# Macaron block (mixture of experts, attention, mixture of experts) on one core: another order of the opening

## The chip, the cores and the metric

The kernel runs on one NeuronCore of a Trainium2 chip. It is one launch; the time is the device time in microseconds of that core, and lower is better. The core has five engines that run side by side, each with its own instruction stream: TensorE (PE) multiplies matrices, VectorE (DVE) and ScalarE (ACT) work element by element and can read the PSUM banks into which TensorE writes, GpSimd (POOL) works element by element on SBUF, and SyncE (SP) issues data transfers (DMAs). An engine takes its instructions in the written order, and waits on semaphores for the others.

## The reference, cut to what matters

`x` has 8 sequences of 1024 tokens with 128 features, in float32. The output is made in three steps.

```
x = x + 0.5 * ffn(layernorm(x))
x = x + attention(layernorm(x))        # causal, one head, d = 128
x = x + 0.5 * ffn(layernorm(x))        # the same weights as in the first

def ffn(f):                            # f: 8192 tokens x 128
    scores = sigmoid(f @ Wg.T)         # 16 experts, in 4 groups of 4
    topk_idx, topk_w = route(scores, bias_corr)   # 2 best groups, in them the 4 best experts,
                                       # weights divided by their sum, times 2.5
    cw = zeros(T, 16).at[..., topk_idx].add(topk_w)
    hid = relu(einsum('th,eih->eti', f, W1)) ** 2     # 64 hidden units per expert
    out = einsum('eth,te->th', einsum('eti,ehi->eth', hid, W2), cw)
    return out + relu(f @ Ws1.T) ** 2 @ Ws2.T         # plus a shared expert of 128 units
```

## The kernel before, in words

All tokens stay in SBUF (`x_sb`: 64 tiles of 128 tokens). An expert phase goes through 16 groups of 4 tiles (512 tokens). The hidden units are cut into 9 chunks of 128: chunks 0 to 7 hold two experts each, chunk 8 is the shared expert. Chunk m counts on over the groups, so that group 2 begins with chunk 18. For each chunk:

- `up` (L1268): TensorE multiplies the chunk of W1 with the group's normalised, transposed tokens. Float32 precision comes from three products of rounded values (`split3`, L1205): high by high, high by low, low by high. There are three PSUM banks for it (HB = 3), so up m waits for gate m - 3.
- `gate` (L950): VectorE takes the positive part and multiplies it with `wb`, the square root of the routing weight of each token, spread over the partitions (L958); for the shared expert there is no weight (L960). Gates of chunks 0 and 4 of a group wait for the two halves of the load of `wb`.
- `square` (L516): ScalarE squares into a rounded high half (L521) and a full one (L522).
- `lo_part` (L380): POOL subtracts the two (L385). Chunk 5 of a group has no such part and is multiplied in full precision (L1280).
- `down` (L1275): TensorE multiplies with the chunk of W2 and adds up in PSUM.

TensorE runs `up` four chunks ahead of `down` (AHEAD = 4). Between them stand the preparing steps of later groups: statistics (L766, L773, L777), a power of -1/2 on POOL for the standard deviation (L368, `inv`) and for the routing sum (L378, `norm_root`), `norm_shift` (L797), `normalise` (L466 on ScalarE, L812 on VectorE), transposes (L1238), a copy to `x_f`, a rounded copy `x_hi` (L452 in both cases: the line of the helper `copy`), `x_lo` on POOL (L391), logits, and the routing in ten parts (L817 to L947; the last writes `scw`, L946). Its result is transposed (L1266), copied to `wT` on ScalarE, stored to memory by SP (L310), and loaded back in a spread form into `wb` (L323): four transfers of 512 KB a group, 2 MB. SP waits for the store to land before it issues the loads, and waits for `wT` of the next group. All of SP's transfers go through one queue.

The opening (on TensorE `opening` at L1295, on ScalarE at L528, on VectorE at L977, on POOL in `start` at L406) prepares groups 0 to 3 and the weights, and starts chunks 0 to 3. SP's queue holds first the tokens of groups 0 and 1, the first weights, groups 2 and 3, then all other tokens in one transfer of 3 MB (L298), then Qw, Kw and Vw; ScalarE's queue holds W2 and Ws2 (L454). TensorE transposes the weights in five sets of four squares (`weights_transpose`, L1211): sets 0 and 1 are W1, 2 and 3 are W2, set 4 is the shared expert and Qw, Kw. ScalarE copies each set from PSUM to a rounded high half (`weights_hi`, L697), and VectorE makes the low half by subtracting that from PSUM (`weights_lo`, L745). Each of groups 1 to 3 has its first two tiles normalised by ScalarE (`first_half`) and the other two by VectorE (`second_half`). The shift of a group can only be written when the tiles of the group before are normalised (L795, and L395 on POOL for the power).

## Time and profile before

| | |
|---|---|
| Time, median of 3 runs | 699.76 us (699.64 to 699.94) |
| The profiled execution's own time | 699.16 us |
| Its span in the profile | 697.4 us |
| TensorE busy | 668.6 us, 96% |
| VectorE busy | 562.0 us, 81% |
| ScalarE busy | 536.0 us, 77% |
| POOL busy | 438.3 us, 63% |
| Moved by DMA | 78.37 MB, 112 GB/s over the span |

Times in the rows are microseconds from the start of the span. A bracket at the end of a row tells for how long the engine did nothing ahead of the instruction, and the arrow which instruction or transfer ended that. SPq and ACTq are the issuing of transfers; a transfer lands later. The first expert phase lasts until about 245 us, attention until about 488 us, the second expert phase until the end.

### The profile page before, as it was taken

To read this page: it belongs to the slowest core of one execution; us is meant where nothing else is said; L and a number is where in the kernel's file an instruction comes from. 1 tells how busy PE (TensorE), PEld (TensorE's weight loads), DVE (VectorE), ACT (ScalarE), POOL (GpSimd) and SP (SyncE) were. 2 spreads that over 40 slices of the span, in tenths; PEclk is the share of its full clock that TensorE was granted. 3 is DMA by queue.
4 is the path that set the end of the run, shared out by engine and by line. 5 is a ranking of instruction groups with operands and counts; after the bars stand their busy time and mean duration, and the time that the engine had idled before them with its cause. 6 is when DMAs were issued, how large, how long until landed. Compare 5 with 4: busy or idle time off the path is not lost.

```text
span 697.4 us, 15216 instructions
## 1 busy us (share of the span) xinstructions
PE 668.6 (96%) x3395; PEld 507.7 (73%) x3395; DVE 562.0 (81%) x2586; ACT 536.0 (77%) x1122; POOL 438.3 (63%) x347
## 2 busy tenths in 40 slices
PE   4789999999999997999999999999999999999997
PEld 3567777777777775787778777767777777777775
DVE  5898988889888885666656678898888899888863
ACT  3479889888898866675566477669898888988975
POOL 3379888989899972000000021148889988999975
PEclk9999999999999999999999999999999999999999
DMA  9867777667775740000000000264887787867783
GB/s 245 195 128 149 151 160 154 126 141 154 162 151 124 157 86 1 1 1 1 0 1 0 0 1 0 57 135 101 167 172 157 166 176 173 166 143 176 162 175 81
DMA packets 53525, 78.37 MB, mean 112 GB/s; under 512 B 5216, under 2 KB 19184, under 8 KB 53488
## 3 DMA queue, kind: packets, MB, share of 16 engines
q1 hardware_dynamic: 51280, 77.36, 51.7%
q10 hardware_dynamic: 2208, 0.59, 0.4%
q8 instruction: 14, 0.23, 0.1%
q14 instruction: 23, 0.19, 0.1%
HBM read 72.70 MB, written 5.24 MB: 112 GB/s over the span
## 4 chain that ended last, share of the span: by engine, by line
PE 76%; DVE 13%; ACT 5%; issue 4%; POOL 1%; DMA 1%; DVEq 0%; POOLq 0%; ACTq 0%
PE psum L1207 19%; PE psum L1208 18%; PE psum L1209 18%; PE psum L1430 6%; PE psum L1280 4%; DVE nmax L1087 3%; PE psum L1238 2%; PE psum L1419 2%; PE psum L1292 2%; ACT shared L630 2%; PE psum L1443 2%; DVE zn L1101 2%; PE psum L1254 1%; DVE s_sb L958 1%; ACT wb L452 1%
## 5 line engine op out<-in xcount | busy, mean ns | idle before, releaser
L385 POOL TENSOR_TENSOR shared_r<-shared,shared_r 128x512 fp32r<-128x512 f32 x256 | 326.7, 1299 | 54.3 <-ACT shared L522 51.7
L958 DVE SCALAR_TENSOR_TENSOR s_sb<-psum,wb 128x512 f32<-128x512 f32 x256 | 175.7, 688 | 46.3 <-DMA wb<-scratch 22.0
L521 ACT ACTIVATE shared_r<-s_sb 128x512 fp32r<-128x512 f32 x256 | 160.2, 626 | 44.1 <-DVE s_sb L958 43.0
L522 ACT ACTIVATE shared<-s_sb 128x512 f32<-128x512 f32 x288 | 178.0, 620 | 18.5 <-DVE s_sb L958 18.5
L1207 PE MATMUL psum<-x_hi,w_hi 128*128 128x512 f32 x288 | 127.6, 443 | 0.9 <-DVE x_sb L1113 0.5
L1207 PE MATMUL psum<-shared_r,w_hi 128*128 128x512 f32 x256 | 114.2, 446 | 0.8 <-POOL shared_r L385 0.7
L1208 PE MATMUL psum<-x_lo,w_hi 128*128 128x512 f32 x288 | 114.7, 398 | 0.0
L1209 PE MATMUL psum<-x_hi,w_lo 128*128 128x512 f32 x288 | 114.3, 397 | 0.0
L1208 PE MATMUL psum<-shared_r,w_hi 128*128 128x512 f32 x256 | 101.0, 395 | 0.0
L1209 PE MATMUL psum<-shared_r,w_lo 128*128 128x512 f32 x256 | 100.9, 394 | 0.0
L368 POOL TENSOR_TENSOR a_rstd<-a_mv,neg_half 128x8 f32<-128x8 f32 x8 | 13.1, 1638 | 116.5 <-DVE a_mv L777 116.5
L1207 PEld LDWEIGHTS psum<-x_hi,w_hi 128*128 128x128 f32 x288 | 54.7, 190 | 20.7 <-issue 7.2
L1208 PEld LDWEIGHTS psum<-x_lo,w_hi 128*128 128x128 f32 x288 | 54.7, 190 | 18.2 <-issue 7.2
L630 ACT ACTIVATE shared<-psum,nmax 128x128 f32<-128x128 f32 (+3 forms) x64 | 47.5, 742 | 23.6 <-DVE nmax L1087 22.3
L1209 PEld LDWEIGHTS psum<-x_hi,w_lo 128*128 128x128 f32 x288 | 54.6, 189 | 13.1
L1087 DVE TENSOR_REDUCE nmax<-psum 128x1 f32<-128x128 f32 (+3 forms) x64 | 47.5, 752 | 19.8 <-PE psum L1410 19.7
L1207 PEld LDWEIGHTS psum<-shared_r,w_hi 128*128 128x128 f32 x256 | 48.2, 188 | 18.7 <-issue 5.5
L466 ACT ACTIVATE xn<-x_sb,shift,roots 128x128 f32 (+1 forms) x128 | 55.6, 482 | 2.8 <-DVE shift L797 2.7
L1209 PEld LDWEIGHTS psum<-shared_r,w_lo 128*128 128x128 f32 x256 | 48.1, 188 | 10.9
L1208 PEld LDWEIGHTS psum<-shared_r,w_hi 128*128 128x128 f32 x256 | 48.6, 190 | 5.0 <-issue 0.2
L404 POOL TENSOR_TENSOR roots<-powers,neg_half 128x8 f32<-128x8 f32 x28 | 45.9, 1638 | 6.4 <-DVE powers L938 5.3
L1430 PE MATMUL psum<-wb,zn 128*128 128x512 f32 (+3 forms) x128 | 47.2, 513 | 0.0
(173 smaller groups left out, 1276.4 us busy)
## 6 DMA issues: line engine op xcount, KB each, us to landing
wb<-scratch SPq DMA_DIRECT2D x128, 512.0 KB, 8.3
out<-x_sb SPq DMA_DIRECT2D x16, 256.0 KB, 9.9
x_sb<-in_L_attn_x SPq DMA_DIRECT2D x4, 256.0 KB, 6.2
scratch<-wT SPq DMA_DIRECT2D x32, 32.0 KB, 1.9
w_raw<-in_L_ffn_W ACTq DMA_DIRECT2D x1, 512.0 KB, 6.0
w_raw<-in_L_ffn_W SPq DMA_DIRECT2D x1, 512.0 KB, 6.7
w_raw<-in_L_ffn_Ws ACTq DMA_DIRECT2D x1, 64.0 KB, 8.7
w_raw<-in_L_ffn_Ws SPq DMA_DIRECT2D x1, 64.0 KB, 7.3
```

Source lines behind the costliest of these rows:

```text
L385: nc.gpsimd.tensor_tensor(g_lo[:, j % RING, :], g_f[:, j % RING, :], g_hi[:, j % RING, :].bitcast(F32), ALU.subtract).then_inc(F.glo_done, 1)
L404: nc.gpsimd.tensor_tensor(roots[:], powers[:], neg_half[:, 0:2 * TG], ALU.pow).then_inc(F.rstd_done, 1)
L466: ins = nc.scalar.activation(xn[:, t, :], x_sb[:, bass.ds(g * TG + t, 1), :].rearrange("p t d -> p (t d)"), ACT.Identity, bias=shift[:, t: ...
L521: nc.scalar.activation(g_hi[:, j % RING, :], s_sb[:, j % RING, :], ACT.Square)
L522: nc.scalar.activation(g_f[:, j % RING, :], s_sb[:, j % RING, :], ACT.Square).then_inc(F.sq_done, 1)
L630: nc.scalar.activation(prob[:, t % PR, 0:w], sc_ps[t % 2][:, 0:w], ACT.Exp, bias=nmax[:, u, t:t + 1], accum_out=rsum[:, u, t:t + 1]).then_ ...
L958: ins = nc.vector.scalar_tensor_tensor(s_, h_, 0.0, wb[:, u, c, :], ALU.max, ALU.mult)
L1087: nc.vector.tensor_reduce(nmax[:, u, t:t + 1], sc_ps[t % 2][:, 0:(t + 1) * P], AX.X, ALU.max, negate=True).then_inc(A.max_done, 1)
L1207: mm(out_, l_hi, r_hi, start=start, stop=False)
L1208: mm(out_, l_hi, r_lo, start=False, stop=False)
L1209: return mm(out_, l_lo, r_hi, start=False, stop=stop)
L1430: ins = mm(u_ps[:, q0:], zn[:, u, k, :], pT[half][:, k, q0:], start=(k == 0), stop=(k == last - 1))
```

## The change

- SP's first transfer (tiles 0 to 3) becomes two of two tiles; the second is issued by ScalarE. W2 and Ws2 move from ScalarE's queue to SP's, behind the tokens of group 3.
- The 3 MB of other tokens become three transfers: group 4 behind Vw; groups 5 and 6 behind the `wb` load of group 0; groups 7 to 15 behind the `wb` load of group 1. VectorE waits for the second before the body of groups 0 and 1 and for the third before the loop that follows.
- `weights_lo` moves from VectorE to POOL. POOL doesn't read PSUM, so ScalarE copies each set once more, unrounded, to SBUF (`wt_f`, in the space of `zn` and `oT`).
- Groups 1 to 3 are normalised by ScalarE alone (`whole_group`).
- TensorE transposes set 4 and the first routing weights earlier, and makes up 0 and 1 ahead of the transposes of group 2, and up 2 ahead of those of group 3. The first down waits for all low halves.
- VectorE, ScalarE and POOL get a new order in the opening.

```diff
@@ -224,6 +224,8 @@
         pT = [w_raw[:, 0:HQ * HQ * P].rearrange("p (k q) -> p k q", k=HQ),
...
         uT = s_sb[:, AHEAD:AHEAD + 2, :]
+        zn_flat = zn[:].rearrange("p u t d -> p (u t d)")
+        wt_f = [zn_flat[:, 512 * w:512 * (w + 1)] for w in range(4)] + [oT[:]]
...
         up_ps = [psum[:, b, :] for b in range(HB)]
@@ -261,8 +263,9 @@
         N_SETS = len(wt_ps)
-        x_in = [sem(f"x_in{g}") for g in range(4)]
-        x_rest = sem("x_rest")
+        x_in = [sem(f"x_in{g}") for g in range(5)]
+        x_rest = [sem(f"x_rest{n}") for n in range(2)]
+        XR = (5, 7, NG)
         wg_in, bias_in, w1_in, w2_in, small_in = sem("wg_in"), sem("bias_in"), sem("w1_in"), sem("w2_in"), sem("small_in")
...
         wgT_done, wgT_copied = sem("wgT_done"), sem("wgT_copied")
@@ -286,7 +289,7 @@
         def _(sp):
-            sp.dma_start(x_sb[:, 0:TG, :], x_v[:, 0:TG, :]).then_inc(x_in[0], 16)
+            sp.dma_start(x_sb[:, 0:TG // 2, :], x_v[:, 0:TG // 2, :]).then_inc(x_in[0], 16)
             sp.dma_start(wg_raw[:], Wg).then_inc(wg_in, 16)
...
             w1_rows = W1.rearrange("e i h -> (e i) h").rearrange("(c p) h -> p c h", p=P)
@@ -295,10 +298,13 @@
             sp.dma_start(bias_bc[:], bias_corr.rearrange("(a e) -> a e", a=1).broadcast_to([P, E])).then_inc(bias_in, 16)
...
                 sp.dma_start(x_sb[:, TG * g:TG * (g + 1), :], x_v[:, TG * g:TG * (g + 1), :]).then_inc(x_in[g], 16)
-            sp.dma_start(x_sb[:, 4 * TG:NT, :], x_v[:, 4 * TG:NT, :]).then_inc(x_rest, 16)
+            sp.dma_start(w2_raw[:, NC, :], Ws2).then_inc(w2_in, 16)
+            sp.dma_start(w2_raw[:, 0:NC, :].rearrange("h c (j i) -> h (c j) i", i=I),
+                         W2.rearrange("e h i -> h e i")).then_inc(w2_in, 16)
             sp.dma_start(qk_raw[:, 0, :], Qw).then_inc(small_in, 16)
...
             sp.dma_start(vw[:], Vw).then_inc(small_in, 16)
+            sp.dma_start(x_sb[:, 4 * TG:5 * TG, :], x_v[:, 4 * TG:5 * TG, :]).then_inc(x_in[4], 16)
...
                 F = FF[phase]
@@ -329,6 +335,9 @@
                     spread(n, n % UN)
+                    if phase == 0 and n < 2:
+                        cs = slice(TG * XR[n], TG * XR[n + 1])
+                        sp.dma_start(x_sb[:, cs, :], x_v[:, cs, :]).then_inc(x_rest[n], 16)
                     if phase == 1 and n == 2 * UN - 1:
...
                 with sp.Fori(2, NG // UN) as i:
@@ -370,6 +379,19 @@
             def attention_inv(b):
...
+            def weights_lo(w):
+                pool.wait_ge(wt_hi, w + 1)
+                flat = lambda a, k: a[:, 4 * k:4 * k + 4, :].rearrange("p c n -> p (c n)")
+                lo_of = lambda lo, hi, f: nc.gpsimd.tensor_tensor(lo, f, hi.bitcast(F32), ALU.subtract)
+                if w < 2:
+                    lo_of(flat(w1_lo, w), flat(w1_hi, w), wt_f[w]).then_inc(wt_lo, 1)
+                elif w < 4:
+                    lo_of(flat(w2_lo, w - 2), flat(w2_hi, w - 2), wt_f[w]).then_inc(wt_lo, 1)
+                else:
+                    lo_of(w1_lo[:, NC, :], w1_hi[:, NC, :], wt_f[w][:, 0:P])
+                    lo_of(w2_lo[:, NC, :], w2_hi[:, NC, :], wt_f[w][:, P:2 * P]).then_inc(wt_lo, 1)
             def ffn(F):
...
@@ -408,15 +430,22 @@
                     inv(1)
...
                         x_lo_part(0, 0)
+                        weights_lo(0)
                         norm_root(0)
                         inv(2)
+                        weights_lo(1)
                     else:
...
                         norm_root(0)
+                    if F is FF[0]:
+                        weights_lo(2)
+                    inv(3)
+                    if F is FF[0]:
+                        weights_lo(3)
+                        weights_lo(4)
                     x_lo_part(1, 1)
-                    inv(3)
                     norm_root(1)
...
                         lo_part(m, m)
@@ -451,9 +480,7 @@
         def _(sc):
...
-            sc.dma_start(w2_raw[:, 0:NC, :].rearrange("h c (j i) -> h (c j) i", i=I),
-                         W2.rearrange("e h i -> h e i")).then_inc(w2_in, 16)
-            sc.dma_start(w2_raw[:, NC, :], Ws2).then_inc(w2_in, 16)
+            sc.dma_start(x_sb[:, TG // 2:TG, :], x_v[:, TG // 2:TG, :]).then_inc(x_in[0], 16)
...
             nc.scalar.activation(warm[:], neg_half[:], ACT.Sigmoid)
@@ -525,6 +552,10 @@
                     for t in range(TG // 2):
...
+                def whole_group(n):
+                    for t in range(TG):
+                        normalise(F, n, t)
                 def opening():
                     first_half(0)
@@ -532,24 +563,24 @@
                     copy(wgT[:, 0:E], lg_ps[:, 0:E]).then_inc(wgT_copied, 1)
...
                     sigmoid(0, 0, lg_ps)
-                    first_half(1)
+                    whole_group(1)
                     x_hi_copy(0, 0)
...
                     weights_hi(2)
+                    wT_copy(0, wT_ps)
                     weights_hi(3)
+                    weights_hi(4)
                     x_hi_copy(1, 1)
-                    wT_copy(0, wT_ps)
-                    first_half(2)
+                    whole_group(2)
                     x_copy(2, 0, tr_ps)
                     sigmoid(2, 0, lg_ps)
-                    weights_hi(4)
-                    first_half(3)
-                    x_copy(3, 1, tr_ps)
+                    whole_group(3)
                     attention_matrix()
                     lead(0)
+                    x_copy(3, 1, tr_ps)
                     wT_copy(1, wT_ps)
...
                         lead(c)
@@ -700,15 +731,18 @@
                 src = wt_ps[w]
...
                 if w < 2:
-                    copy(flat(w1_hi, w), src).then_inc(wt_hi, 1)
+                    copy(flat(w1_hi, w), src)
+                    copy(wt_f[w], src).then_inc(wt_hi, 1)
                 elif w < 4:
...
                             copy(w2_f[:, n, :], src[:, (c % 4) * P:(c % 4 + 1) * P])
-                    copy(flat(w2_hi, w - 2), src).then_inc(wt_hi, 1)
+                    copy(flat(w2_hi, w - 2), src)
+                    copy(wt_f[w], src).then_inc(wt_hi, 1)
                 else:
...
                     copy(w2_hi[:, NC, :], src[:, P:2 * P])
+                    copy(wt_f[w][:, 0:2 * P], src[:, 0:2 * P])
                     copy(qkT[:].rearrange("p c n -> p (c n)"), src[:, 2 * P:4 * P]).then_inc(wt_hi, 1)
             def attention_matrix():
@@ -741,19 +775,6 @@
             nc.vector.memset(scw[:, E:, :], 0.0).then_inc(FF[0].stat, 1)
...
             v.wait_ge(FF[0].stat, n_const)
-            def weights_lo(w):
-                v.wait_ge(wt_hi, w + 1)
-                src = wt_ps[w]
-                flat = lambda a, k: a[:, 4 * k:4 * k + 4, :].rearrange("p c n -> p (c n)")
-                if w < 2:
-                    tt(flat(w1_lo, w), src, f32(flat(w1_hi, w)), ALU.subtract).then_inc(wt_lo, 1)
-                elif w < 4:
-                    tt(flat(w2_lo, w - 2), src, f32(flat(w2_hi, w - 2)), ALU.subtract).then_inc(wt_lo, 1)
-                else:
-                    tt(w1_lo[:, NC, :], src[:, 0:P], f32(w1_hi[:, NC, :]), ALU.subtract)
-                    tt(w2_lo[:, NC, :], src[:, P:2 * P], f32(w2_hi[:, NC, :]), ALU.subtract).then_inc(wt_lo, 1)
...
@@ -977,30 +998,25 @@
                 def opening():
                     def statistics(n):
-                        v.wait_ge(x_in[n], 16)
+                        v.wait_ge(x_in[n], 32 if n == 0 else 16)
                         stats(n, range(TG))
...
                     statistics(1)
-                    second_half(1)
+                    norm_shift(1)
                     v.wait_ge(bias_in, 16)
...
                     route_parts(0, 9)
-                    weights_lo(0)
-                    weights_lo(1)
-                    second_half(2)
+                    route_parts(1, 0, 1)
+                    norm_shift(2)
                     statistics(3)
-                    route_parts(1, 0, 1)
-                    weights_lo(2)
-                    weights_lo(3)
-                    second_half(3)
-                    route_parts(1, 2)
-                    weights_lo(4)
-                    route_parts(1, 3, 4, 5, 6, 7, 8)
-                    v.wait_ge(x_rest, 16)
+                    route_parts(1, 2, 3, 4)
+                    norm_shift(3)
+                    route_parts(1, 5, 6, 7, 8)
+                    v.wait_ge(x_in[4], 16)
                     for c in range(AHEAD):
...
@@ -1057,7 +1073,11 @@
                             extra(j)
                 def run(first_extra, last_extra):
+                    if phase == 0:
+                        v.wait_ge(x_rest[0], 16)
                     body(0, True, False, first_extra)
+                    if phase == 0:
+                        v.wait_ge(x_rest[1], 16)
                     if phase == 1:
...
                     with v.Fori(1, NG // UN - 1) as i:
@@ -1275,6 +1295,8 @@
                 def down(g, c, m, j, u):
...
                         wait(pe, F.oT_copied, g - 1)
+                        if phase == 0 and isinstance(g, int) and g == 0:
+                            pe.wait_ge(wt_lo, N_SETS)
                     if c in WHOLE:
...
                         mm(o_ps[u], w2_f[:, WHOLE.index(c), :], g_f[:, j % RING, :], start=(c == 0),
@@ -1306,20 +1328,23 @@
                     xn_transpose(1, tr_ps)
...
                     weights_transpose(2)
+                    w_transpose(0, wT_ps, sigmoids=2)
                     weights_transpose(3)
-                    w_transpose(0, wT_ps, sigmoids=2)
+                    weights_transpose(4)
+                    pe.wait_ge(wt_lo, 1)
+                    pe.wait_ge(wt_hi, 2)
+                    lead(0)
+                    lead(1)
                     pe.wait_ge(F.xf_done, 2)
...
                     logits(2, 0, lg_ps, wT_copied=1)
-                    weights_transpose(4)
+                    pe.wait_ge(wt_hi, N_SETS)
+                    lead(2)
+                    attention_matrix()
                     pe.wait_ge(F.xf_done, 3)
                     xn_transpose(3, tr_ps)
-                    pe.wait_ge(wt_hi, N_SETS)
-                    pe.wait_ge(wt_lo, N_SETS)
-                    attention_matrix()
-                    for c in range(AHEAD - 1):
-                        lead(c)
                     w_transpose(1, wT_ps, sigmoids=3)
+                    pe.wait_ge(wt_lo, 2)
                     pe.wait_ge(m_copied, 2)
...
```

## Rows read from the trace of the kernel before

**Rows 1.** Busy time by stages: us, then per engine busy (instructions), PEclk, DMA share, GB/s

```profile
34.80:43.00 8.20, 6.16 (x33) 3.96 (x31) 7.95 (x54) 5.05 (x10) 5.41 (x6) 1.00 0.66 143
43.00:245.00 202.00, 201.75 (x991) 154.04 (x992) 180.33 (x900) 179.54 (x380) 182.72 (x141) 1.00 0.70 147
```

**Rows 2.** Waits of TensorE, 43 to 245 us, and its timeline where that begins

```profile
PE psum L1259 <- ACT lgT L452: 1.9, 2, 1.7
...
42.89 0.33 PE L1259 MATMUL psum<-ident,lgT 128*128 128x128 f32 x1 [1.66 <-ACT lgT L452]
```

**Rows 3.** Timeline of the opening: start, duration, engine, line, instruction, count

```profile
4.74 0.87 DVE L766 BATCH_NORM_STATS2 bn<-x_sb 128x6 f32<-128x128 f32 x4 [1.31 <-DMA x_sb<-in_L_attn_x]
...
19.32 0.26 DVE L946 SCALAR_TENSOR_TENSOR scw<-psum,roots 128x64 f32<-128x64 f32 x1
...
19.64 0.48 PE L1266 MATMUL psum<-ident,scw 128*128 128x128 f32 x1 [0.32 <-DVE scw L946]
...
20.53 0.26 ACT L452 ACTIVATE wT<-psum 64x128 f32<-64x128 f32 x1
...
20.82 0.55 SPq L310 DMA_DIRECT2D scratch<-wT  x1
...
23.96 2.64 SPq L323 DMA_DIRECT2D wb<-scratch  x4
```

**Rows 4.** Timeline and lines: what moves between engines, and where gate 1 stands

```profile
13.77 0.58 ACT L452 ACTIVATE w_hi<-psum 128x512 fp32r<-128x512 f32 x1
...
20.72 1.26 POOL L391 TENSOR_TENSOR x_lo<-x_f,x_hi 128x512 fp32r<-128x512 f32 x1 [0.22 <-ACT x_hi L452]
...
20.84 0.88 ACT L466 ACTIVATE xn<-x_sb,shift,roots 128x128 f32<-128x128 f32 x2
20.84 1.48 DVE L812 TENSOR_SCALAR xn<-x_sb,roots,shift 128x128 f32<-128x128 f32 x2
...
24.71 1.28 DVE L753 TENSOR_TENSOR w_lo<-psum,w_hi 128x512 fp32r<-128x512 f32 x2
...
33.19 0.68 DVE L958 SCALAR_TENSOR_TENSOR s_sb<-psum,wb 128x512 f32<-128x512 f32 x1
...
L812 DVE TENSOR_SCALAR xn<-x_sb,roots,shift x16: 334/344/1223, 7.6 to 452.8; 128x128 f32<-128x128 f32 x16
...
L933 DVE SCALAR_TENSOR_TENSOR chosen<-marked,scores x32: 217/419/1241, 17.2 to 656.7; 128x64 f32<-128x64 f32 x32
```

**Rows 5.** Busy time by short stretches, for the DMA columns at the end

```profile
10.00:20.00 10.00, 8.53 (x37) 7.58 (x37) 7.63 (x58) 4.86 (x12) 3.56 (x4) 1.00 1.07 292
35.00:36.00 1.00, 1.00 (x6) 0.82 (x5) 1.00 (x7) 0.59 (x2) 0.33 (x1) 1.00 0.37 71
47.00:48.00 1.00, 1.00 (x7) 0.76 (x6) 0.99 (x7) 1.00 (x3) 0.57 (x2) 1.00 0.88 162
```

**Rows 6.** Timeline: stores and loads of groups 1 and 2, gate 18, down 19

```profile
34.58 0.52 SPq L310 DMA_DIRECT2D scratch<-wT  x1
36.88 3.09 SPq L323 DMA_DIRECT2D wb<-scratch  x4
51.05 0.52 SPq L310 DMA_DIRECT2D scratch<-wT  x1
52.92 2.57 SPq L323 DMA_DIRECT2D wb<-scratch  x4
...
60.70 0.69 DVE L958 SCALAR_TENSOR_TENSOR s_sb<-psum,wb 128x512 f32<-128x512 f32 x1
...
68.34 0.50 PE L1207 MATMUL psum<-shared_r,w_hi 128*128 128x512 f32 x1
```

**Rows 7.** Timeline: a first gate of a group that is late

```profile
148.38 0.69 DVE L958 SCALAR_TENSOR_TENSOR s_sb<-psum,wb 128x512 f32<-128x512 f32 x1 [1.70 <-DMA wb<-scratch]
...
150.34 1.30 POOL L385 TENSOR_TENSOR shared_r<-shared,shared_r 128x512 fp32r<-128x512 f32 x1 [1.62 <-ACT shared L522]
...
152.85 5.07 POOL L385 TENSOR_TENSOR shared_r<-shared,shared_r 128x512 fp32r<-128x512 f32 x4
```

## What the change does to the time: the prediction

> **What bounds the kernel now.** I read the busy time by stages first. From 43 us to the end of the first expert phase TensorE is busy for 201.75 of 202.00 us [rows 1], and all that it waits for there is 1.9 us behind one copy of ScalarE, nearly all of it once, ahead of 42.89 us [rows 2]. So from about 43 us on the kernel is a fixed amount of TensorE work, and the end moves by as much as TensorE is earlier or later at any place after that. Before it, in 34.8 to 43 us, VectorE is busy for 7.95 of 8.20 us and TensorE for 6.16 [rows 1]: the opening is paced by VectorE. The diff touches the opening and the loads. An opening that is x us shorter is worth x us, if nothing behind it is late. I therefore read next what must be on time behind it: the broadcast loads of the routing weights (wb, 2 MB a group), one after another in SP's queue. Their times were 23.96, 36.88 and 52.92 us [rows 3, 6].
>
> I call gate m the VectorE instruction that makes the gated activation of chunk m (9 chunks a group), up m the product that it reads and down m the product that needs it. Gate 18 is the first of group 2.
>
> **The change part by part.**
>
> *First tokens in two halves, W2 away from ScalarE's queue.* VectorE could start at 3.4 us, and starts at 4.74 because it waited 1.31 us for 256 KB that shared the engines with 512 KB of W2 [rows 3]. Alone, this data should land earlier. Bounds: 0 and 1.3 us; I take 0.9, since transfers run at up to 292 GB/s [rows 5], so that removing some 250 KB of interleaved data is worth 0.9.
>
> *The chain to the first wb load.* VectorE's part (statistics, routing of group 0, `scw` at 19.32) keeps its order. The copy of wT stood behind x_hi_copy(1) and ran at 20.53, though the transpose of `scw` was done at 20.12 [rows 3]. Now it stands behind weights_hi(2), which by the copy's 0.58 us [rows 4] ends about when the transpose does: 0.3 us gained. The store then goes out at 20.82 - 0.9 - 0.3 = 19.6. In the trace it took until 23.96 because 3 MB of tokens were ahead of it in the queue; with an empty queue it takes 51.05 to 52.92, 1.9 us [rows 3, 6]. So the first wb load is issued at **21.5** in place of 23.96.
>
> *Low halves of the weights on POOL.* Off VectorE go four subtractions of 0.64 us (1.28 for two) and two small ones, some 3.1 us; with them six normalise instructions [rows 4]. ScalarE gets the six (0.44 us each, 0.88 for two) and five copies more of 0.58 or less, some 5.2 us. POOL gets five instructions of up to 1.3 us, a time that its subtraction shows at that size [rows 4], some 5.9 us, and norm_root(1) and inv(3) now stand behind them. Both lists fit in the opening, with the order below. down of chunk 0 waits for all of them, over 5 us after they are done by this count.
>
> *Where this puts gate 1.* ScalarE after wT_copy(0) at 19.5: 0.7 wait, weights_hi(3) and (4) 2.5, x_hi 0.6, four normalises 1.6: 24.9. Then transposes of group 2, copy, logits, sigmoid 3.9: 28.8; four normalises and the copies of the attention matrix 2.5: 31.3; VectorE's m_lo 0.3. Gate 1 is at 31.6 in place of 33.19 [rows 4]. On POOL inv(3) starts at 24.9, then three subtractions and norm_root(1) end at 30.2, so it is no later. From gate 1 on VectorE's list is the old one, so the whole of TensorE's stream would be **1.6 us earlier**. Bounds: nothing (POOL and ScalarE just late enough) and 3 us (all of VectorE's relief).
>
> *Up products ahead of two groups' transposes.* TensorE is not the limit there, so placing up 0 to 2 early gives nothing by itself and costs nothing: they fill its waits.
>
> *A port rule.* Beside a POOL subtraction some VectorE instructions stretch: two normalises took 1.48 us against 0.60, one of them up to 1223 ns against a median of 344, and L933, which reads two SBUF tiles, has 217 to 1241 ns [rows 4]. The Trainium skill, "SBUF — State Buffer", section "SBUF: two separate sides", says why: VectorE's two-port modes, or its instructions with two SBUF inputs, and a GpSimd instruction hold a shared pair of ports exclusively, each for a whole instruction. The trace agrees. It speaks against the change, because weights_lo(0) (about 15.0 to 16.3) ends just where L933 of group 0 falls (16.3), on the chain to the first wb load; by that rule it could lose up to 1.3 us. In the sum I count none and put 1.3 into the upper bound; the normalises that lost 1.1 us are now ScalarE's.
>
> *The tokens behind the wb loads.* Here the cost is. Groups 7 to 15, 36 tiles or 2.36 MB, are issued straight behind the load of group 1, and the store and load of group 2 stand behind them in the same queue. The queue works in order: the store at 34.58 was not in before 36.88, 1.5 us after the last bytes of group 0's load (flow tails off at 35.4) [rows 5, 6]. The count:
> - group 0's load flows until 11.4 us after its issue (23.96 to 35.4) [rows 3, 5]: 32.9. Half a megabyte of tokens behind it at 292 GB/s: 34.7. The store of group 1, issued by 33.5, lands 1.5 later: 36.2 (36.88 before).
> - group 1's load flows until 11.0 after its issue (36.88 to 47.9) [rows 5, 6]: 47.2. Then 2.36 MB at 288 GB/s: 8.2 us, 55.4. Before, the engines were idle here until 52.9. The store of group 2, issued since 49.5, lands at 56.9.
> - gate 18 can run 7.8 us after the issue (52.92 to 60.70) [rows 6]: **64.7**. Before: 60.70, with the load just in. So it is 4.0 us later than before.
>
> *What that costs.* The trace has a late gate of this kind: 148.38, waiting on the load. POOL's low half followed at 150.34, after it the x_lo of the next group and the low half of chunk 19, whose successor starts at 152.85 + 1.25 [rows 7]. So down 19 can't start before gate 18 + 5.9 (with 0.15 for the signal). In group 2 it starts at 68.34 [rows 6], 7.6 after its gate: 1.7 us of slack beyond the 5.9. New start: 64.7 + 5.9 = 70.6, **2.3 us later than before**. This is not added to the 1.6: TensorE comes to this place 1.6 us early, waits 3.9, and leaves 2.3 late. The load of group 3 follows its own store about 10 us after it, moves along with the engines and adds nothing.
>
> **Sum.** The profiled execution took 699.16 us for a span of 697.4; with +2.3 it is 701.4. The median of the runs, 699.76, is 0.6 above the profile: 702.0. Taking the bounds together (the first load 0.4 earlier to 2.2 later, transfers 0.5 us either way, the slack 0.5 either way) the likeliest case alone is 700.8 to 704.6.
>
> **Rivals.**
> 1. *The loads are in time* and only the opening counts: 1.6 us, 698.2 (with its bounds 696.8 to 699.8). For it: the count needs seven legs in a row, and gate 18 may slip 1.7 us free. If the legs come out 4 us shorter (packets of the two transfers overlapping, tokens quicker at 2.36 MB), TensorE never waits. Against: engines are already at a share of 1.07 while moving tokens [rows 5], so nothing overlaps for free.
> 2. *Both nearly cancel:* the late load costs back about the gain, which it does if the first wb load is issued near 19.5 or if the store of group 2 is issued ahead of part of the tokens. End within 1.4 us of before: 699.8.
> 3. *POOL makes the opening longer* (the other side even with loads in time): ports held on VectorE at each of the five subtractions, and norm_root(1) behind x_lo(1). It decides when norm_root(1) ends after 31.8 (its old start) plus 1; five holds of up to 1.2 us would push gate 1 to 34.5 and, through the store of group 1, everything in the count by 2 us more: 704.
> 4. *The change doesn't do what it says:* the first tokens land no sooner, since the delay is latency and not bandwidth. Then all of it is 0.9 later: 702.9, inside the range.
>
> **Chances.** Likeliest case with rival 4: 0.50. Rival 1: 0.22. Rival 2: 0.20. Rival 3: 0.08. A measurement of this kernel tells 0.2% (1.4 us) from no change. Slower by more: most of the first and the third, 0.52; within: 0.26; faster by more: 0.22. Predicted 701.9 us, with the range 697.8 to 704.6.
>
> **What would show it.** Right: first statistics near 3.8 us; store of group 0 near 19.6, its load issued near 21.5; gate 1 near 31.6; x_sb's last transfer landing at 55 or later and SP's load of group 2 issued near 57; a wait of VectorE on wb of 3 us or more ahead of gate 18 near 64.7, and a wait of TensorE of 3 to 4 us near 65 to 70. Wrong: the load of group 2 issued before 55, no wait of TensorE behind 43 us, or gate 1 later than 33.

## The result, and the profile after

The changed kernel takes 703.83 us (median of 8 runs, 701.78 to 705.05), the kernel before beside it 699.82 us (8 runs, 698.47 to 700.71): a ratio of 1.005 with a 95% interval of 1.0033 to 1.0067, so 2.3 to 4.7 us slower; the two medians are 4.0 us apart. It was run once more later, against more runs of before: 1.0045 (1.003 to 1.006). The profiled execution took 705.05 us for a span of 703.2 us; it is the slowest of the eight. The prediction said 701.9, in 697.8 to 704.6.

Lines have moved by some twenty: the gate is L979, the three `up` products L1227 to L1229, the pair that begins `down` of chunk 5 L1302, the store L316, the `wb` load L329.

First the opening, which answers to [rows 3, 4]. This is the timeline of the kernel after (start, duration, engine, line, instruction, count, and in brackets the idle time before it and what ended it):

```profile
3.71 0.87 DVE L787 BATCH_NORM_STATS2 bn<-x_sb 128x6 f32<-128x128 f32 x4 [0.29 <-DMA x_sb<-in_L_attn_x]
...
19.12 0.27 ACT L481 ACTIVATE wT<-psum 64x128 f32<-64x128 f32 x1
...
19.42 0.59 SPq L316 DMA_DIRECT2D scratch<-wT  x1
21.32 2.68 SPq L329 DMA_DIRECT2D wb<-scratch  x4
24.05 0.84 SPq L340 DMA_DIRECT2D x_sb<-in_L_attn_x  x1
...
29.14 0.69 DVE L979 SCALAR_TENSOR_TENSOR s_sb<-psum,wb 128x512 f32<-128x512 f32 x1 [1.22 <-DMA wb<-scratch]
30.08 0.69 DVE L979 SCALAR_TENSOR_TENSOR s_sb<-psum,wb 128x512 f32<-128x512 f32 x1
...
39.78 0.33 PE L1279 MATMUL psum<-ident,lgT 128*128 128x128 f32 x1 [1.51 <-ACT lgT L481]
```

The first four rows are as predicted (3.8, then 19.6 for the store and 21.5 for the load). Gate 1 is at 30.08 and not 31.6, and TensorE's wait for `lgT`, the last of the opening, ends at 39.78 where it ended at 42.89 [rows 2]: the opening is 3.1 us shorter, not 1.6.

Then the loads behind it, answering to [rows 6], and the busy time by stretches (per engine busy time and instructions in the order TensorE, its weight loads, VectorE, ScalarE, POOL; then TensorE's granted clock, DMA share, GB/s), answering to [rows 1]:

```profile
36.71 2.59 SPq L329 DMA_DIRECT2D wb<-scratch  x4
39.76 0.78 SPq L340 DMA_DIRECT2D x_sb<-in_L_attn_x  x1
47.93 5.43 SPq L316 DMA_DIRECT2D scratch<-wT  x1
57.18 2.60 SPq L329 DMA_DIRECT2D wb<-scratch  x4
...
64.76 0.69 DVE L979 SCALAR_TENSOR_TENSOR s_sb<-psum,wb 128x512 f32<-128x512 f32 x1 [7.31 <-DMA wb<-scratch]
```

```profile
34.80:43.00 8.20, 6.69 (x35) 4.96 (x35) 7.75 (x48) 5.85 (x13) 6.57 (x6) 1.00 0.63 141
43.00:245.00 202.00, 197.53 (x958) 150.22 (x957) 172.83 (x869) 173.73 (x369) 176.15 (x136) 0.98 0.73 154
49.00:56.00 7.00, 7.00 (x40) 5.28 (x39) 6.26 (x33) 6.07 (x13) 7.00 (x6) 1.00 1.06 289
60.00:65.00 5.00, 1.46 (x9) 0.89 (x7) 0.24 (x1) 0.00 (x0) 0.00 (x0) 0.96 1.05 214
65.00:71.00 6.00, 5.49 (x13) 4.33 (x14) 5.83 (x37) 5.51 (x12) 4.29 (x4) 0.50 0.62 120
```

TensorE lost 4.5 us in a phase where it had lost 0.25. From 49 to 56 us the engines move tokens at 289 GB/s, and the store of group 2, issued at 47.93, is behind them (its issuing alone takes 5.43 us, 0.52 in before [rows 6]): its load goes out at 57.18 (predicted 56.9), and gate 18 runs at 64.76 (predicted 64.7). The last row holds what was not predicted: from 65 to 71 us the granted clock is 0.50, the lower of its two levels (1.2 of 2.4 GHz). TensorE's timeline shows what that is in matmuls:

```profile
61.06 0.40 PE L1229 MATMUL psum<-shared_r,w_lo 128*128 128x512 f32 x1
65.51 0.79 PE L1227 MATMUL psum<-x_hi,w_hi 128*128 128x512 f32 x1 [4.05 <-DVE s_sb L979]
66.10 0.63 PE L1228 MATMUL psum<-x_lo,w_hi 128*128 128x512 f32 x1
66.53 0.63 PE L1229 MATMUL psum<-x_hi,w_lo 128*128 128x512 f32 x1
...
70.79 0.63 PE L1227 MATMUL psum<-x_hi,w_hi 128*128 128x512 f32 x1
71.22 0.52 PE L1228 MATMUL psum<-x_lo,w_hi 128*128 128x512 f32 x1
71.58 0.39 PE L1229 MATMUL psum<-x_hi,w_lo 128*128 128x512 f32 x1
71.89 0.43 PE L1274 MATMUL psum<-x_f,wgT 128*32 128x128 f32 x8
72.25 0.50 PE L1227 MATMUL psum<-shared_r,w_hi 128*128 128x512 f32 x1
```

Behind the wait of 4.05 us the matmuls start 0.43 us apart, until 71.2; then 0.23 again. The last row is down 19, at 72.25: 3.9 us later than before [rows 6], where 2.3 was predicted.

One place serves as a marker in every run below: the start of `down` of chunk 5, the only matmul in two products. In TensorE's timeline it starts for groups 0, 1 and 2 at 45.85, 60.22, 74.58 before, and at 42.73, 57.11, 78.48 after: 3.1 early, 3.1 early, 3.9 late. For the last group it is 688.77 and 694.69, 5.9 late. A group takes 14.35 us, and nine of the thirteen profiles, that of before too, have single groups that take 0.5 to 1.2 more, at other places in each (before, group 8 starts 14.85 after group 7). The 3.9 grow by 2.0 to the 5.9. Two such groups in the kernel after and one in before make 0.7 of that, 0.6 come between 237 and 494 us, 0.5 in the last groups. In the second profile of the changed kernel (below) it is 3.8 at the end.

What makes a group slow can be read from the timeline, here that of before between the markers of groups 7 and 8:

```profile
155.66 1.07 DVE L933 SCALAR_TENSOR_TENSOR chosen<-marked,scores 128x64 f32<-128x64 f32 x1
156.66 0.68 DVE L958 SCALAR_TENSOR_TENSOR s_sb<-psum,wb 128x512 f32<-128x512 f32 x1
157.37 0.63 ACT L522 ACTIVATE shared<-s_sb 128x512 f32<-128x512 f32 x1 [1.23 <-DVE s_sb L958]
157.91 0.26 ACT L452 ACTIVATE lgT<-psum 128x128 f32<-128x128 f32 x1
158.22 0.33 PE L1259 MATMUL psum<-ident,lgT 128*128 128x128 f32 x1 [0.25 <-ACT lgT L452]
```

L933, a step of the routing that reads two SBUF tiles, starts inside the third of four POOL subtractions in a row [rows 7] and takes 1.07 us where it can take 0.22. The gate behind it is late, ScalarE waits 1.23 us for the gate, its copy `lgT` is late, and TensorE waits. Of the groups that have a routing, 16 in all profiles together take 14.8 us or more without a late load; each of these has this instruction at 0.66 to 1.26 us and a wait of TensorE for `lgT` of 0.20 to 0.54. The reverse doesn't hold: the instruction also takes up to 1.40 us in groups of 14.35.

### The profile page after: what moved, and what is told of

It reads as the page before. It is cut to its first block, busy times and chain, and to the rows that moved or that the text cites. A ratio compares the mean times of both kernels' runs of the same rounds, so it can differ in the third digit from the quotient of the medians.

```text
span 703.2 us, 15219 instructions
## 1 busy us (share of the span) xinstructions
PE 672.4 (96%) x3395; PEld 509.4 (72%) x3395; DVE 558.4 (79%) x2574; ACT 539.6 (77%) x1133; POOL 443.4 (63%) x353
## 4 chain that ended last, share of the span: by engine, by line
PE 64%; DVE 13%; DMA 8%; ACT 6%; issue 5%; POOL 2%; SPq 0%; DVEq 0%; POOLq 0%; ACTq 0%
PE psum L1227 16%; PE psum L1228 15%; PE psum L1229 15%; PE psum L1455 6%; DMA wb<-scratch 5%; PE psum L1302 3%; DVE nmax L1107 2%; DVE s_sb L979 2%; DMA scratch<-wT 2%; PE psum L1444 2%; ACT shared L661 2%; PE psum L1468 2%; PE psum L1258 2%; PE psum L1314 2%; DVE zn L1121 1%
## 5 line engine op out<-in xcount | busy, mean ns | idle before, releaser
L979 DVE SCALAR_TENSOR_TENSOR s_sb<-psum,wb 128x512 f32<-128x512 f32 x256 | 175.2, 687 | 53.9 <-DMA wb<-scratch 32.7
L1227 PE MATMUL psum<-x_hi,w_hi 128*128 128x512 f32 x288 | 128.6, 446 | 4.4 <-DVE s_sb L979 4.0
L1227 PE MATMUL psum<-shared_r,w_hi 128*128 128x512 f32 x256 | 115.1, 450 | 1.2 <-POOL shared_r L407 1.2
L1229 PE MATMUL psum<-x_hi,w_lo 128*128 128x512 f32 x288 | 115.3, 400 | 0.0
L1229 PE MATMUL psum<-shared_r,w_lo 128*128 128x512 f32 x256 | 101.6, 397 | 0.0
L1227 PEld LDWEIGHTS psum<-x_hi,w_hi 128*128 128x128 f32 x288 | 55.2, 192 | 23.9 <-issue 6.7
L661 ACT ACTIVATE shared<-psum,nmax 128x128 f32<-128x128 f32 (+3 forms) x64 | 47.4, 741 | 23.1 <-DVE nmax L1107 21.9
L1229 PEld LDWEIGHTS psum<-x_hi,w_lo 128*128 128x128 f32 x288 | 55.1, 191 | 13.2
L1227 PEld LDWEIGHTS psum<-shared_r,w_hi 128*128 128x128 f32 x256 | 48.7, 190 | 19.0 <-issue 5.0
L493 ACT ACTIVATE xn<-x_sb,shift,roots 128x128 f32 (+1 forms) x134 | 57.8, 483 | 4.1 <-DVE shift L818 4.1
L1229 PEld LDWEIGHTS psum<-shared_r,w_lo 128*128 128x128 f32 x256 | 48.6, 190 | 11.1
```

The costliest lines, as they stand in the source:

```text
L493: ins = nc.scalar.activation(xn[:, t, :], x_sb[:, bass.ds(g * TG + t, 1), :].rearrange("p t d -> p (t d)"), ACT.Identity, bias=shift[:, t: ...
L661: nc.scalar.activation(prob[:, t % PR, 0:w], sc_ps[t % 2][:, 0:w], ACT.Exp, bias=nmax[:, u, t:t + 1], accum_out=rsum[:, u, t:t + 1]).then_ ...
L979: ins = nc.vector.scalar_tensor_tensor(s_, h_, 0.0, wb[:, u, c, :], ALU.max, ALU.mult)
L1227: mm(out_, l_hi, r_hi, start=start, stop=False)
L1229: return mm(out_, l_lo, r_hi, start=False, stop=stop)
```

## The experiments

The theory after the result: *the late load of group 2 makes the kernel slower, and hides an opening that is 3.1 us shorter*. The rival: *something else of the change costs it*, VectorE's or POOL's new lists, or the clock. All times are given beside before on the same chip. The first four ran beside 27 runs of before with a median of 701.9 us, 5 to 8 beside 29 with 700.69, 9 to 11 beside 22 with 700.23; so ratios are compared, and the markers.

**1. Tokens in the gaps.** The change, with groups 5 to 11 moved into the idle queue of the opening, group 12 behind load 0 and only 13 to 15 behind load 1.

```diff
-        XR = (5, 7, NG)
+        XR = (5, 12, 13, NG)
...
             sp.dma_start(x_sb[:, 4 * TG:5 * TG, :], x_v[:, 4 * TG:5 * TG, :]).then_inc(x_in[4], 16)
+            sp.dma_start(x_sb[:, TG * XR[0]:TG * XR[1], :], x_v[:, TG * XR[0]:TG * XR[1], :]).then_inc(x_rest[0], 16)
```

> The changed kernel with its tokens placed elsewhere: groups 5 to 11 straight behind group 4, in the stretch from 12.4 to 19.4 us in which its trace moves nothing, group 12 behind the load of group 0, groups 13 to 15 (0.79 MB, 2.7 us) behind the load of group 1. Theory L (the late load of group 2 is the whole loss): the store of group 2 lands about when it did before relative to the engines, gate 18 near 58, no wait of TensorE of over 0.5 us behind 43 us, granted clock 1.00 from 35 us on; the opening's 3.1 us stay: 696.7 us, ratio to before 0.9955. Rival O (POOL and ScalarE, loaded with more, cost later, and the load only covers it): 699 to 703 us.

Measured: 698.99 us, ratio 0.9973 (0.9956 to 0.999), the profiled execution 697.94. The load of group 2 and gate 18 in its timeline:

```profile
50.30 2.58 SPq L330 DMA_DIRECT2D wb<-scratch  x4
...
58.06 0.69 DVE L980 SCALAR_TENSOR_TENSOR s_sb<-psum,wb 128x512 f32<-128x512 f32 x1 [0.50 <-DMA wb<-scratch]
```

Nothing else was changed, and TensorE no longer waits there; the clock is 1.00 from 34 us on. The marker is 3.0 us earlier than before in all of the first groups (42.84, 57.22, 71.57). Of that 1.2 are left at the last group of the profile (687.58 against 688.77), behind groups of 14.92, 15.11 and 14.69 us; the ratio forecast, 0.9955, was not reached. So the kernel that was slower becomes faster, by the place of one transfer alone. That shows the theory's first half.

**2. Before, with the tokens late and nothing else** (group 4 alone in the opening, 5 and 6 behind load 0, 7 to 15 behind load 1, and the waits for them).

```diff
-            sp.dma_start(x_sb[:, 4 * TG:NT, :], x_v[:, 4 * TG:NT, :]).then_inc(x_rest, 16)
+            sp.dma_start(x_sb[:, 4 * TG:5 * TG, :], x_v[:, 4 * TG:5 * TG, :]).then_inc(x_in[4], 16)
...
                     spread(n, n % UN)
+                    if phase == 0 and n < 2:
+                        cs = slice(TG * XR[n], TG * XR[n + 1])
+                        sp.dma_start(x_sb[:, cs, :], x_v[:, cs, :]).then_inc(x_rest[n], 16)
```

> The kernel before with one part of the change alone: group 4 behind group 3, groups 5 and 6 behind the load of group 0, groups 7 to 15 behind the load of group 1. Theory L: store of group 0 lands at 22.7 in place of 23.96, the store of group 2 at about 58, gate 18 near 65.7 against 60.7; TensorE waits some 2 us ahead of up 21. If its clock stays at 1.00 the end is 3.3 us later (703.1), if the wait drops it to 0.5 for as long as in the changed kernel, 4.8 us later (704.6). Rival O: within 1 us of before, since engines have their old lists.

Measured: 705.49 us, ratio 1.0072 (1.0043 to 1.0101); marker 45.65, 60.03, 78.71, the last 4.1 late. The load of group 2 went out at 57.97. The wait by itself is 2.5 us, and here too the clock falls, 1.5 us after TensorE has started again, and stays low until 71.4:

```profile
66.88 0.50 PE L1215 MATMUL psum<-x_hi,w_hi 128*128 128x512 f32 x1 [2.50 <-DVE s_sb L962]
67.22 0.40 PE L1216 MATMUL psum<-x_lo,w_hi 128*128 128x512 f32 x1
...
68.15 0.43 PE L1217 MATMUL psum<-shared_r,w_lo 128*128 128x512 f32 x1
68.38 0.63 PE L1215 MATMUL psum<-x_hi,w_hi 128*128 128x512 f32 x1
```

So the tokens' place costs 4 us by itself. The profiled execution, 702.63 us, is the fastest of the five. As ratios the two expectations are 1.0047 (clock kept) and 1.0068 (clock lost): the second is met, the first isn't excluded.

**3. The wait filled.** The change, with 34 transposes of the identity, written where nothing is read any more, ahead of up 21: TensorE works through its wait. They are extra work, 3.87 us in all.

```diff
+                                if phase == 0 and first and j == UN * NCH - 1:
+                                    for _ in range(34):
+                                        nc.tensor.transpose(o_ps[0][:, 0:P], ident[:], ident[:])
                                 up(g + 1, (c + AHEAD) % NCH, m + AHEAD, (j + AHEAD) % (UN * NCH), 0)
```

> The changed kernel, and in the 4 us wait ahead of up 21 TensorE makes 34 transposes that nobody reads (3.7 us by 0.11 us each), into a bank that is free then. Theory L with the clock: the time of the wait is the load's and stays, but TensorE's granted clock stays at 1.00 in 65 to 71 us, where the changed kernel has 0.50, so down 19 comes 2.7 us sooner: 701.1 us against 703.8. Rival (the 6.7 us from up 21 to down 19 are POOL's chain and not the clock): at least 1.7 us of them stay and the time is 702.8 or more.

Measured: 704.06 us, ratio 1.0054 (1.0033 to 1.0075), the profiled execution 703.68. The same stretch of TensorE:

```profile
61.75 3.87 PE L1381 MATMUL psum<-ident 128*128 128x128 f32 x34
65.38 0.47 PE L1227 MATMUL psum<-x_hi,w_hi 128*128 128x512 f32 x1
65.69 0.40 PE L1228 MATMUL psum<-x_lo,w_hi 128*128 128x512 f32 x1
...
69.85 0.43 PE L1274 MATMUL psum<-x_f,wgT 128*32 128x128 f32 x8 [0.43 <-ACT x_f L481]
70.24 0.50 PE L1227 MATMUL psum<-shared_r,w_hi 128*128 128x512 f32 x1
```

The clock stays at 1.00, and down 19 is at 70.24 behind a gate 18 at 64.43: 5.8 us, the predicted distance of 5.9. In the kernel after it was 7.5. But the marker of group 2 is at 77.24, only 1.2 ahead of the kernel after, and 0.36 of that is a load that went out earlier. From down 19 to the marker it is 6.24 us in before and 6.23 in the kernel after, and 7.00 here, because this group is one of the slow ones: L954 takes 1.05 us at 71.73, and TensorE waits for `lgT`:

```profile
74.27 0.33 PE L1279 MATMUL psum<-ident,lgT 128*128 128x128 f32 x1 [0.53 <-ACT lgT L481]
```

The times don't tell the two apart: the intervals 1.0033 to 1.0075 and 1.0033 to 1.0067 lie on each other. At the marker 0.9 us of the low clock's cost came back. With the usual 6.24 the marker would be at 76.5, so I estimate its cost at 1.6 us; whether the slow group stands there in every execution, one profile doesn't tell. The expected 701.1 was wrong: with the clock back the marker is still 2.7 us later than before (1.9 by that estimate), and a group of 15.47 us comes later.

**4. All tokens ahead of the first store.** The change, with groups 5 to 15 as one transfer in the opening.

```diff
+            sp.dma_start(x_sb[:, 5 * TG:NT, :], x_v[:, 5 * TG:NT, :]).then_inc(x_rest[0], 16)
...
-                    if phase == 0 and n < 2:
-                        cs = slice(TG * XR[n], TG * XR[n + 1])
-                        sp.dma_start(x_sb[:, cs, :], x_v[:, cs, :]).then_inc(x_rest[n], 16)
```

> The changed kernel with all tokens of groups 5 to 15 ahead of the first store, as the kernel before has them. Theory L: the store of group 0, issued at 19.4, lands behind them near 23.9, the first gate is at 31.7 in place of 29.1, later loads are in time, no wait behind 43 us. Of the opening's 3.1 us some 0.5 are left: 699.3 us. Rival O: 702 us or more.

Measured: 703.87 us, ratio 1.003 (1.0007 to 1.0052); a miss. Store and load of group 0, the gate behind them, and two stretches of five:

```profile
19.30 3.00 SPq L317 DMA_DIRECT2D scratch<-wT  x1
26.00 2.65 SPq L330 DMA_DIRECT2D wb<-scratch  x4
...
33.99 0.69 DVE L977 SCALAR_TENSOR_TENSOR s_sb<-psum,wb 128x512 f32<-128x512 f32 x1 [6.17 <-DMA wb<-scratch]
```

```profile
10.00:15.00 5.00, 4.06 (x19) 3.29 (x18) 3.40 (x29) 3.80 (x10) 1.44 (x2) 1.00 0.66 166
28.00:34.00 6.00, 1.08 (x4) 0.71 (x4) 0.01 (x1) 1.02 (x4) 1.48 (x2) 0.50 1.05 223
```

Before, the engines moved 292 GB/s from 10 to 20 us [rows 5]; here it is 166 from 10 to 15, while SP's queue is at W2, whose transfer now stands in it. The expectation took over the 23.9 of before; the tokens end later, the store is behind them, and the load goes out at 26.00, 4.7 after the kernel after. TensorE waits 5.3 us for `scw` and works at the lower clock until about 41 us. The marker of group 2 (76.31) is 1.7 late. It is a second case of the same fault, at another group.

**5 to 8. One part of experiment 1 taken back in each**, to find what the 3.0 us come from.

*5: the first tokens whole on SP again, W2 and Ws2 on ScalarE's queue.*

```diff
-            sp.dma_start(x_sb[:, 0:TG // 2, :], x_v[:, 0:TG // 2, :]).then_inc(x_in[0], 16)
+            sp.dma_start(x_sb[:, 0:TG, :], x_v[:, 0:TG, :]).then_inc(x_in[0], 16)
...
-            sc.dma_start(x_sb[:, TG // 2:TG, :], x_v[:, TG // 2:TG, :]).then_inc(x_in[0], 16)
+            sc.dma_start(w2_raw[:, 0:NC, :].rearrange("h c (j i) -> h (c j) i", i=I),
+                         W2.rearrange("e h i -> h e i")).then_inc(w2_in, 16)
```

> e1_tokens_in_gaps with one part undone: tiles 0 to 3 in one transfer of SP, W2 and Ws2 in ScalarE's queue again. All is told in the start of down 5 in group 0 (45.85 us in the kernel before, 42.84 in e1). Theory F (the first tokens land 1.0 us sooner and the whole chain moves with it): first statistics at 4.7, down 5 at 43.8, time 1.0 us over e1. Rival (the latency sets it, W2's traffic doesn't): first statistics at 3.7 and down 5 at 42.8.

Measured: 700.46 us, ratio 0.9988 (0.9971 to 1.0005); statistics begin at 4.57, load 0 at 22.16, marker 44.32: 1.5 us lost of the 3.0 (1.0 was expected). The edit takes back both the halves and the queue of W2, and doesn't tell them apart.

*6: the low halves on VectorE again* (`weights_lo` reads PSUM, and ScalarE's second copies go).

```diff
-                        weights_lo(0)
                         norm_root(0)
                         inv(2)
-                        weights_lo(1)
...
-                    copy(flat(w1_hi, w), src)
-                    copy(wt_f[w], src).then_inc(wt_hi, 1)
+                    copy(flat(w1_hi, w), src).then_inc(wt_hi, 1)
...
+                    weights_lo(0)
+                    weights_lo(1)
                     route_parts(1, 0, 1)
```

> e1_tokens_in_gaps with the low halves on VectorE again, from PSUM, without ScalarE's five copies for POOL. VectorE stands idle for 2.5 us ahead of 25.35 in the changed kernel, so its 3.1 us fit there almost wholly, and ScalarE's chain gets 2.4 us shorter. Theory C (ScalarE's and TensorE's chain to m_hi sets gate 1, not VectorE's work): down 5 at 42.8 or sooner, down to 42.2. The reason of the prediction (relief of VectorE by POOL brings the gain): down 5 at 44.4 or later.

Measured: 698.06 us, ratio 0.9963 (0.9944 to 0.9983); marker 43.14, 0.3 later than experiment 1.

*7: groups 1 to 3 normalised by ScalarE and VectorE again.*

```diff
-                    whole_group(1)
+                    first_half(1)
...
-                    norm_shift(1)
+                    second_half(1)
```

> e1_tokens_in_gaps with groups 1 to 3 normalised half by ScalarE, half by VectorE, as the kernel before. Two sides: ScalarE's chain gets 3 x 0.8 us shorter, VectorE gets 6 x 0.34 us and holds of up to 1.2 us where POOL works beside. Theory C: down 5 between 42.2 and 43.2. If the VectorE load counts: 44.0 or later.

Measured: 696.67 us, ratio 0.9956 (0.9929 to 0.9984); marker 42.83, as experiment 1. So each time VectorE has work back on its list, and the marker moves by 0.3 us or not at all.

*8: up 0 to 2 behind the transposes of group 3.*

```diff
                     weights_transpose(4)
-                    pe.wait_ge(wt_lo, 1)
-                    pe.wait_ge(wt_hi, 2)
-                    lead(0)
-                    lead(1)
                     pe.wait_ge(F.xf_done, 2)
...
-                    lead(2)
...
                     xn_transpose(3, tr_ps)
+                    pe.wait_ge(wt_lo, 1)
+                    lead(0)
+                    lead(1)
+                    lead(2)
```

> e1_tokens_in_gaps with up 0, 1 and 2 behind the transposes of group 3. The prediction gave their early place no value. Theory K (they bring TensorE's granted clock up before the transposes and logits of group 2, which take 0.63 and 1.07 us in the changed kernel against 1.09 and 1.89 before, and are out of the way of gates 0 to 2): these take 1.1 and 1.9 us again, down 5 at 44.2 or later, time 1.3 us or more over e1. Rival (no value): down 5 at 42.8 to 43.2.

Measured: 701.42 us, ratio 1.0011 (0.9992 to 1.0031); marker 47.84, 5.0 later than experiment 1 and 2.0 later than before. By the ratios that is some 2.7 us more than experiment 1. Its gate 0, TensorE's transposes and logits of group 2, and the place ahead of the marker:

```profile
24.34 1.09 PE L1260 MATMUL psum<-ident,xn 128*128 128x128 f32 x4 [3.50 <-ACT xn L494]
26.12 1.89 PE L1268 MATMUL psum<-wgT,x_f 128*128 128x16 f32 x8 [0.69 <-ACT x_f L482]
...
32.45 0.69 DVE L980 SCALAR_TENSOR_TENSOR s_sb<-psum,wb 128x512 f32<-128x512 f32 x1 [4.47 <-PE psum L1231]
...
43.33 0.33 PE L1281 MATMUL psum<-ident,lgT 128*128 128x128 f32 x1 [1.66 <-ACT lgT L482]
43.97 0.59 PE L1231 MATMUL psum<-shared_r,w_lo 128*128 128x512 f32 x1
44.35 0.63 PE L1229 MATMUL psum<-x_hi,w_hi 128*128 128x512 f32 x1
```

VectorE now waits 4.47 us for the up product, and the wait for `lgT` ends at 43.33, 3.4 later than in experiment 1 (39.88) and 0.4 later than before: without the early up products the whole rest of the change gains nothing in the opening. The pace of transposes and logits, which the expectation put first, is the small part: experiment 1 has 0.63 and 1.89 us there, and its scores of group 2 start 0.6 earlier (27.43 against 28.04). The other 1.6 of the 5.0 are matmuls 0.43 us apart from 43.97 to 47.4, a fall of the clock that experiment 1 doesn't have at that place.

**9 and 10. To go below.** Experiment 1's gate 0 waits 1.01 us for the first half of its load. In 9 that half comes in two pieces, with a semaphore for chunks 0 and 1; 10 takes 9, 6 and 7 together.

```diff
+                    if phase == 0 and isinstance(n, int) and n == 0:
+                        for e in range(P // I):
+                            src = scratch[phase, bass.ds(n, 1)].rearrange("n (c e) t -> (n e) c t", e=P // I)[e:e + 1, 0:2, :]
+                            sp.dma_start(wb[e * I:(e + 1) * I, u, 0:2], src.broadcast_to([I, 2, GT])).then_inc(w_first, 16)
```

> e1_tokens_in_gaps, and the first half of group 0's load in two pieces (chunks 0 and 1, then 2 and 3), gate 0 waiting for the first, gate 2 for the second. Theory: in e1 gate 0 waits 1.0 us for the load (28.84); it comes at 27.9 now, but gate 1 stands behind scw of group 1 and m_lo, which POOL's norm_root(1) and ScalarE's m_hi release near 29.5. So gate 1 near 29.9 against 30.18, down 5 at 42.5, time within 0.4 us of e1. If gate 0's wait was all: gate 1 at 29.2, down 5 at 41.9.

> e9_first_quarter with the low halves on VectorE (e6) and the shared normalising (e7) too. POOL has no low halves ahead of norm_root(1), ScalarE's chain is 4 us shorter, so m_hi and scw are ready when gate 0 is done. If the wait on the load was what hid it in e6 (1.99 us) and e7: gate 0 near 27.7, gate 1 near 28.8, down 5 near 41.6, 1.2 us under e1. If VectorE's own work takes its place: down 5 at 42.5 to 44.

Measured: 696.96 us, ratio 0.9956 (0.9941 to 0.9971), and 696.79 us, 0.9956 (0.9938 to 0.9974). In 9 gate 0 runs at 27.80 without a wait and gate 1 at 29.89, but the wait for `lgT` ends at 39.59, a mere 0.3 earlier, and in this profile the clock falls behind it:

```profile
36.00:40.00 4.00, 1.97 (x8) 1.01 (x7) 3.90 (x25) 1.95 (x4) 2.89 (x3) 0.99 0.98 213
40.00:44.00 4.00, 4.00 (x12) 3.15 (x11) 3.05 (x15) 3.90 (x9) 3.73 (x3) 0.59 1.07 207
```

Nine matmuls 0.36 to 0.43 us apart in place of 0.23: the marker is at 44.11, 1.3 after experiment 1 (expected 42.5). In 10 it is at 42.98, not 41.6: gate 0 runs at 28.80 without a wait on the load, as late as in experiment 1, since VectorE's own work stands ahead of it. That is the expectation's second case. An earlier first gate alone (9) brings 0.3 us at `lgT`. Versions 7, 9 and 10 are the fastest, all three at 0.9956 and with intervals below 1: they beat before by some 3 us and the changed kernel by some 6. Neither among themselves nor from experiments 1 and 6 are they told apart.

**11. The changed kernel again**, unchanged, on the chip of 9 and 10, as a reference for them.

> The changed kernel itself once more, beside the others on the same chip. Its ratio to before is 1.0055 again (1.005 measured first); down 5 of group 0 at 42.7, of group 2 at 78.5, gate 18 near 64.8.

Measured: 703.38 us, ratio 1.0045 (1.003 to 1.006); load 2 at 57.09, gate 18 at 64.89, marker 42.73, 57.11, 77.47. All this repeats, but the clock does so only in part: it is low from 65.6 to 69.4 and not to 71.2, and down 19 starts at 71.23, 1.0 earlier than in the first profile.

## Why the prediction was right, and where not

Its result holds: slower, inside the range, by the mechanism named. The size was low: 2.1 us were forecast, 3.5 (by the ratio) to 4.0 (by the medians) were found. By its own steps:

- *First tokens land sooner* (3.8): 3.71. *The chain to the first load* (19.6, 21.5): 19.42, 21.32. Right; experiment 5 puts the worth of the first transfers at 1.5 us of the opening.
- *The tokens behind the loads* (store 2 landed 56.9, gate 18 at 64.7): 57.18 and 64.76, 57.09 and 64.89. The count of seven legs, bytes ahead in the queue by GB/s, was off by 0.3 us at its end, and by 0.5 at most on the way (load 1 at 36.71, with 36.2 forecast). Experiments 1 and 2 show from both sides that this, with the wait's fall of the clock, is the whole loss up to the marker of group 2.
- *Gate 18 plus 5.9* (down 19 at 70.6): 72.25 and 71.23, and 70.24 with the wait filled. The rule held, and the step failed that let TensorE come out of its wait at full pace. In the profile this is 0.6 to 1.7 us over the forecast; of the 2.0 between 72.25 and 70.24, experiment 3 shows 0.9 at the marker (77.24, where 74.58 + 2.3 = 76.9 was forecast), and 1.6 by the estimate without its slow group.
- *Up products ahead of two groups' transposes: gives nothing and costs nothing.* Wrong, the largest mis-sized term: put at nothing. The prediction looked at TensorE's busy share before 43 us and took VectorE's list as the limit. Gate 0 needs up 0 and gate 1 needs up 1. Behind the transposes of group 3, which wait for ScalarE, these products, three matmuls of 0.43 us each, release the gates only at 32.45 and 33.63 (experiment 8); ahead of them they are long done, and gate 0 waits for its load only. Taking this away costs 3.4 us at `lgT`, as much as the whole gain of the opening. The 1.5 us of experiment 5 don't add to it: each is what is lost when that part alone is missing.
- *VectorE's relief gives 1.6 us* (low halves to POOL, normalising to ScalarE): experiments 6 and 7 find 0.3 us and nothing, and 10, with both back, 0.4 at `lgT` against 9. The reading that VectorE paces the opening, since it is busy for 7.95 of 8.20 us, was the wrong step. (The normalises lost 0.9 us, 1.48 against 0.60, and not the 1.1 of the prediction.) POOL's cost, rival 3, isn't there either: the subtraction ran from 14.89 to 16.16, and L954 of group 0, L933 before, started at 16.20 and took 0.22 us. So the port rule of the prediction (the Trainium skill, "SBUF — State Buffer", section "SBUF: two separate sides") had no occasion there. The hold was missed by 0.04 us; over the kernel L954 has 218 to 1343 ns, so holds go on elsewhere, and the slow groups shown above are what they can cost.
- *Rival 1* (in time, 698.2) is what experiment 1 is, with 3.0 in place of 1.6: 699.16 - 3.0 = 696.2, against 697.94 in its profile, where single slow groups took the rest. *Rival 2* (both nearly cancel, within 1.4 us): the interval, 2.3 to 4.7 us, excludes it, and neither of its conditions holds, the first load being issued at 21.32 and the store of group 2 behind all tokens. *Rival 4*: excluded by 3.71.

Together at the marker of group 2: forecast 2.3 late, found 3.9 and 2.9. The opening's 1.5 us more didn't help, as the forecast said of its own 1.6: what TensorE gains ahead of a wait only lengthens the wait.

What stays open: why a long L954 delays TensorE in some groups and not in others, what makes the 0.6 us between 237 and 494 us and the 0.5 in the last groups, and whether other executions have them. No kernel was made for it.

## What to carry to other kernels

Count a queue by bytes: what stands ahead of a small, urgent transfer in the same queue delays it by its bytes over the measured GB/s, and that sum was right to 0.5 us here, though some 2 us short where W2 stood in the queue (experiment 4). Moving a large transfer out of an idle time is no saving; place it where the queue is idle and nothing urgent follows (experiment 1 against the change: some 5 us). And before an instruction placed early is priced at nothing, ask which engine's next wait it ends: the idle engine's last product was what the busy one had to wait for.

## What the runs showed of the hardware beyond that

- A wait of TensorE may cost more than its length. Behind waits of 4.05 and 4.17 us the matmuls started 0.43 us apart for 5.7 and 3.8 us; behind one of 2.50 us the clock fell 1.5 us later, for 3 us; behind the one of 1.5 to 1.7 us for `lgT` that eleven of the thirteen profiles have at 40 to 43 us it fell in experiments 8 and 9 and stayed in the nine others. The same program had it at two lengths (experiment 11). With the wait filled by transposes it didn't fall.
- The granted clock reads 1.00 in the opening of before, while up products start 0.43 us apart there (30.4 to 33.9 us) and 0.23 after. A stretch's clock column alone doesn't tell the pace; the starts of equal matmuls do.
- One queue gave 292 GB/s with tokens and 166 in the stretch that holds W2's transfer (experiment 4). Over the same 10 to 15 us it gave 165 in experiment 6 and 241 in experiment 1, with W2 at the same place, and 298 in experiment 5, with W2 on ScalarE's queue. That speaks for W2; that the size of its pieces is the reason wasn't tried by itself.
